# A macaron block: both expert layers as one group of eight steps, two biases moved, the last joins shared by two engines

## The chip, the cores and the metric

One core of a Trainium2 chip runs the whole program in one launch. The metric is the device time of an execution in microseconds (us), here always of that one core; a lower time is better. The engines are TensorE (PE), VectorE (DVE), ScalarE (ACT), GpSimd (POOL) and SyncE (SP). SP and POOL issue the transfers between device memory and the core.

## The reference

Input: 32 tiles of 128 tokens (8 sequences of 512), 128 features, f32.

```python
x = x + 0.5 * ffn(layernorm(x))           # layer 0
x = x + attention(layernorm(x))
x = x + 0.5 * ffn(layernorm(x))           # layer 1, the same weights

# ffn: a second layernorm, then top 2 of 8 experts per token by softmax(normed @ router.T);
#   each expert: silu(gate) * up @ down, 384 wide; and a shared expert, 128 wide, for all tokens
# attention: windows of 128 tokens; q, k, v = x @ W.T + b; scores q k / sqrt(128); in each row the
#   32 largest of 128 scores kept, softmax, times v; leaky relu; + its input; layernorm * gamma + beta
```

## The kernel before

**Steps and blocks.** The 32 tiles are worked on in 8 steps of 4 tiles (`TB`). In a step of an expert layer the router picks two experts for each token, VectorE works out a row number for each of the 1024 (token, expert) pairs (`s_idx`, line 1316), and POOL scatters the normed tokens to those rows of a table `rows` in device memory, eight indirect transfers for a step (line 1726), so that the rows of one expert stand together. The expert's work is then done in blocks of 128 rows of one expert: SP loads the rows (line 519) and the expert's weights (line 522); TensorE transposes (line 793), multiplies for gate (800), up (809) and down (820); ScalarE copies the transpose (1049), makes silu of the gate (1052) and copies the output (1058); VectorE multiplies silu by up (1543); POOL scatters the 128 output rows to `results` (line 1747). A block has four parts (0 transpose, 1 gate, 2 up, 3 down), and each engine has those of its own.

**Lists and groups.** Which expert a block belongs to is known only at run time. VectorE writes lists of blocks (`block_list`, lines 1373 to 1429) from the counts of the steps so far, and `level` (1364) keeps the counts at the steps named in `LEVELS`, by which a list is put in order, so that results of early steps come early. A list can be worked on once the steps it covers are scattered (`begin`, line 482). `GROUPS` says which steps share a region of `rows`: a group pays for one partly filled block for each expert, so its last list has seven blocks more than the rows need at best. `FIRST`, the first block of each list, comes to 0, 31, 78, 87, ..., 127, 149: layer 0 has a list of 31 blocks (steps 0 to 2) and one of 47 (steps 3 to 7), layer 1 seven lists with 71 blocks. `RUNS` are the places where the pipeline of blocks is drained: 31, 78 and the end. At a group's end SP writes pads over the unfilled rows (`fill_all`, 529; `fill_spare`, 465). Outputs stand in 12 buffers (`YB`); the load of block B waits until the result of block B - 12 is scattered.

**The order.** Every engine runs a written order. Between the pieces of the routing and attention steps stands a call `turn()`, and the numbers in `WEAVE` say for each engine how many block parts it does at each call (`z3` is three calls with none). For TensorE: first the eight routing steps of layer 0 (`first_turn` to `first_prefixes`), then for s in `TURNS` a step that holds, for four tiles each, attention of step a, the rest of attention of step a - 1 (`turn_p`, `mix`), routing of layer 1 of step a - 2 (`turn_z`, line 655, `logits`, `prefixes`), and the transpose of the next step's attention input (`turn_x`, line 647). What is left of the blocks comes behind all steps (`turn.rest()`).

**Around the change.** After layer 0's blocks of some steps are stored, SP loads their results (`stored`, `results`, lines 539 and 559), ScalarE multiplies the rows by their gates (`gate_rows`, line 956, a turn behind each second row) and VectorE adds them to the stream (`combine`, line 1457). `values` (TensorE, line 694) multiplies by the weights; VectorE adds the bias `bv_b` to a 128x512 tile (line 1500). `biased` adds the bias of attention's last norm to the stream (POOL, line 1737, ahead of that step's routing scatters). At the end of layer 1 all results of steps 0 to 6 are weighted by ScalarE and added by VectorE; those of the last step are weighted and added in one operation on VectorE (`last_joins`, line 1461).

Of the kernel before, what the change touches and what calls it, by code (L numbers as in the profile page):

```python
# [120 lines left out]
for now, f in zip(SHARED_AT, TURNS):  # L121
# [23 lines left out]
        z160 1 z4 1 z6 1 z5 1 z3 1 z3 1 z2 1 z4 1 z8 1 z5 1 z7 1 z4 1 z1 1 z5 2 z7 1 z2 1 z2 1 z3 1 z7 1 z1 1 z1 3 14 z5 1 z10 2 z1 1 z1 1 z10 1 2
        z16 1 z12 1 z3 1 z7 1 z6 1 z2 1 z4 1 z13 1 z18 2 1 z8 1 z7 1 z1 1 z6 1 z5 1 z15 1 1 z28 1 z4 1 z6 1 z15 2 z20 1 z24 1 z14 1 z2 1 1 z5 1 z10
        1 z4 1 z22 1 z40 1 z2 1 z15 1 z1 1 z9 1 z17 1 z7 1 z21 1 z1 1 z15 1 1 z15 1 z7 1 z1 1 1 z25 1 z2 1 z31 1 z1 1 z5 1 z16 1 z5 1 z2 1 z5 1 z16
        1 z18 1 z16 1 1 z7 1 z12 1 z4 1 z7 1 z30 1 z15 1 z5 1 z8 1 z11 2 1 z31 1 z2 1 z7 1 z4 2 z4 2 z1 3 16 3 2 z2 1 z10""",
# [6 lines left out]
VALUES, AFTER, AFTER_LATE, PICKS, SHARED, SHARED_LATE = 8, 13, 12, 19, 26, 31  # L155
# [48 lines left out]
def macaron(nc, x, wq, bq, wk, bk, wv, bv, ga, ba, gf, bf, rw, guw, dnw, sguw, sdnw, out, xs, yt):  # L204
    ctx = ExitStack()
    with ctx:
# [150 lines left out]
        cb, gated = sem("cb"), sem("gated")  # L357
# [569 lines left out]
        def _(act):  # L927
# [57 lines left out]
            def mix(A):  # L985
# [141 lines left out]
            for J in range(LAST_LO):  # L1127
                gate_rows(STEPS + J, yg_of(STEPS + J), J * TB)
# [10 lines left out]
        def _(dve):  # L1139
# [483 lines left out]
            for s, f in enumerate(TURNS):  # L1623
# [8 lines left out]
                if R is not None:  # L1632
                    stats_route(R, Jr, rt)

                def between(m):
# [3 lines left out]
                    if m == VALUES and a is not None:  # L1639
                        values(a)  # L1640
# [147 lines left out]
```

## Time and profile before

| | us |
|---|---|
| median of three executions | 546.54 |
| lowest, highest | 544.11, 551.48 |
| the profiled execution | 548.3 |
| its span in the profile | 546.5 |
| TensorE busy | 468.9 |
| VectorE busy | 368.8 |
| ScalarE busy | 348.1 |
| POOL busy | 288.6 |

The page gives the busy time of each engine over the whole span; the timeline gives single instructions with the idle time of the engine before them and, in brackets, what ended it; the windows cut the span into stretches with the busy time of each engine and the clock that TensorE was granted there (1.00 is 2.4 GHz, half of it 1.2 GHz; a value between is a mean of the stretch). Times are counted from the start of the span.

### The profile page before, as it was taken

How to read it: one execution, taken by the hardware profiler on the slowest of the kernel's cores; microseconds unless marked ns; L12 is line 12 of the kernel's file. 1: busy time of each engine (PE TensorE's matmuls, PEld its weight loads, DVE VectorE, ACT ScalarE, POOL GpSimd, SP SyncE). 2: the span in 40 equal slices, each digit the busy share in tenths (PEclk: the TensorE clock that was granted, in tenths of full speed). 3: DMA queues.
4: the chain of work that ended last, by engine and by line, in shares of the span. 5: the costliest groups of instructions: out<-in, count | busy, mean ns of one | idle time of the engine just before them, and what ended most of it. 6: DMA issues, size and time to landing. Idle time of an engine off the chain costs nothing.

```text
span 546.5 us, 13689 instructions
## 1 busy us (share of the span) xinstructions
PE 468.9 (86%) x3662; PEld 427.8 (78%) x3662; DVE 368.8 (67%) x1660; ACT 348.1 (64%) x870; POOL 288.6 (53%) x320
## 2 busy tenths in 40 slices
PE   2496799889997999999989989989998999699960
PEld 1483699888897879798868778887978898699960
DVE  5455654574225578888999989999999967222245
ACT  3374356547458568677887776868665565655586
POOL 2357367777731543233474736284685777544431
PEclk9999798999999999999999989999999999999995
DMA  6962485667658545352844366455554456767787
GB/s 170 303 168 88 169 277 189 213 194 264 230 191 300 188 158 172 139 192 95 271 146 160 108 231 185 160 179 171 170 184 165 158 211 214 257 236 260 244 289 235
DMA packets 79399, 108.42 MB, mean 198 GB/s; under 512 B 10888, under 2 KB 54288, under 8 KB 79328
## 3 DMA queue, kind: packets, MB, share of 16 engines
q1 hardware_dynamic: 68048, 88.33, 48.7%
q0 software_dynamic: 8864, 18.24, 10.2%
q10 hardware_dynamic: 2416, 0.99, 0.8%
q8 instruction: 34, 0.56, 0.4%
q14 instruction: 37, 0.30, 0.2%
HBM read 25.64 MB, written 23.29 MB: 90 GB/s over the span
## 4 chain that ended last, share of the span: by engine, by line
PE 44%; DVE 23%; issue 9%; ACT 9%; DMA 8%; SPq 4%; POOL 1%; ACTq 0%; DVEq 0%; POOLq 0%
PE ps_y L820 10%; PE ps_g L800 10%; PE ps_u L809 5%; PE ps_h L809 5%; DMA raw_dn<-in_dnw 3%; DVE raw_gu L1543 2%; DVE scores L1520 2%; PE w L686 2%; ACT yg L956 2%; DVE top L1515 2%; PE ps_x L793 2%; DVE bn L1163 2%; DMA yg<-results 2%; SPq L475 2%; DMA results<-raw_gu 2%
## 5 line engine op out<-in xcount | busy, mean ns | idle before, releaser
L1747 POOL DMA_INDIRECT results<-raw_gu x149 | 147.5, 990 | 133.6 <-ACT raw_gu L1058 96.1
L1726 POOL DMA_INDIRECT rows<-zz,s_idx x128 | 125.7, 982 | 93.1 <-issue 48.9
L820 PE MATMUL ps_y<-dn_t,raw_gu 128*128 x894 | 128.1, 280 | 10.5 <-ACT raw_gu L1058 9.7
L800 PE MATMUL ps_g<-x_t,raw_dn 128*128 128x128 f32 x894 | 127.3, 279 | 0.0
L820 PEld LDWEIGHTS ps_y<-dn_t,raw_gu 128*128 128x128 f32 x894 | 113.1, 193 | 17.6 <-issue 17.3
L800 PEld LDWEIGHTS ps_g<-x_t,raw_dn 128*128 128x128 f32 x894 | 113.7, 194 | 2.2 <-issue 2.2
L1052 ACT ACTIVATE sil<-ps_g 128x384 f32<-128x384 f32 x149 | 73.3, 492 | 17.5 <-PE ps_g L800 16.9
L1058 ACT COPY raw_gu<-ps_y 128x128 f32<-128x128 f32 x149 | 39.4, 264 | 69.2 <-PE ps_y L820 68.8
L1049 ACT ACTIVATE x_t<-ps_x,bf_c,gf_c 128x128 f32<-128x128 f32 x149 | 68.9, 462 | 21.8 <-PE ps_x L793 21.8
L1543 DVE TENSOR_TENSOR raw_gu<-sil,ps_h 128x384 f32<-128x384 f32 x74 | 40.7, 550 | 49.5 <-PE ps_h L809 34.9
L809 PE MATMUL ps_u<-x_t,raw_dn 128*128 128x128 f32 x450 | 64.1, 280 | 2.3 <-DVE raw_gu L1543 2.3
L1543 DVE TENSOR_TENSOR raw_gu<-sil,ps_u 128x384 f32<-128x384 f32 x75 | 41.2, 550 | 36.8 <-PE ps_u L809 30.2
L809 PE MATMUL ps_h<-x_t,raw_dn 128*128 128x128 f32 x444 | 62.1, 276 | 0.0
L809 PEld LDWEIGHTS ps_u<-x_t,raw_dn 128*128 128x128 f32 x450 | 58.0, 196 | 5.0 <-DVE raw_gu L1543 3.1
L809 PEld LDWEIGHTS ps_h<-x_t,raw_dn 128*128 128x128 f32 x444 | 55.8, 192 | 2.3 <-issue 1.7
L793 PE MATMUL ps_x<-ident,raw_gu 128*128 128x128 f32 x149 | 41.7, 280 | 12.3 <-DMA raw_gu<-rows 11.5
L973 ACT ACTIVATE zz<-xres,nmr,rstd 128x256 f32<-128x256 f32 x64 | 34.8, 595 | 8.7 <-DVE nmr L1230 8.7
L1515 DVE MAX8 top<-scores 128x8 f32<-128x128 f32 x128 | 35.3, 285 | 0.8 <-ACT scores L1019 0.8
L1520 DVE MATCH_REPLACE8 scores<-top,scores 128x128 f32<-128x128 f32 x128 | 34.9, 275 | 0.0
L793 PEld LDWEIGHTS ps_x<-ident,raw_gu 128*128 128x128 f32 x149 | 21.5, 144 | 16.3 <-issue 14.8
L956 ACT ACTIVATE yg<-yg,gates 128x128 f32<-128x128 f32 x96 | 30.8, 400 | 4.1 <-DMA yg<-results 4.1
L1457 DVE TENSOR_TENSOR xres<-xres,yg 128x512 f32<-128x512 f32 x24 | 16.9, 705 | 12.1 <-ACT yg L956 11.7
(228 smaller groups left out, 690.9 us busy)
## 6 DMA issues: line engine op xcount, KB each, us to landing
raw_dn<-gu_t SPq DMA_DIRECT2D x149, 384.0 KB
raw_gu<-rows SPq DMA_DIRECT2D x149, 64.5 KB, 2.8
yg<-results SPq DMA_DIRECT2D x12, 512.0 KB, 4.3
results<-raw_gu POOLq DMA_INDIRECT x149
rows<-zz,s_idx POOLq DMA_INDIRECT x128
out<-xres SPq DMA_DIRECT2D x7, 256.0 KB, 3.5
rows<-pads SPq DMA_DIRECT2D x24, 64.5 KB
raw_dn<-in_dnw SPq DMA_DIRECT2D x1, 1536.0 KB, 15.1
```

The source lines that it names most:

```text
L793: pe.transpose(ps_x[:, 0, :], xin[:, kx, 0:D], ident[:]).then_inc(xT_ps, 1)
L800: t = pe.matmul(ps_g[k][:, c, :], ws[:, k4, c * P:(c + 1) * P], x_t[:, k, :], start=True, stop=True)
L809: t = pe.matmul(ps_us[k][:, c, :], ws[:, k4, FF + c * P:FF + (c + 1) * P], x_t[:, k, :], start=True, stop=True)
L820: t = pe.matmul(ps_y[:, 0, :], h_t[:, k4, c * P:(c + 1) * P], dn[:, bass.ds(off + c * D, D)], start=(c == 0), stop=(c == FC - 1))
L956: act.activation(yg[n][:, k, c, :], yg[n][:, k, c, :], ACT.Copy, scale=gates[:, c, tile + k:tile + k + 1]).then_inc(gated, 1)
L1049: act.activation(x_t[:, k, :], ps_x[:, 0, :], ACT.Identity, bias=bf_c[:], scale=gf_c[:]).then_inc(xT_sb, 1)
L1052: act.activation(sil[:, B % 3, :], ff(ps_g[k]), ACT.Silu).then_inc(sil_done, 1)
L1515: dve.max(top[:, k, eight], src[:, k, :]).then_inc(tk, 1)
L1520: dve.match_replace(wk_s[:, k, :], top[:, k, eight], src[:, k, :], TAKEN).then_inc(tk, 1)
L1543: dve.tensor_tensor(h_t[:, k4, :], sil[:, B % 3, :], ff(ps_us[k]), ALU.mult).then_inc(h_done, 1)
L1726: pool.indirect_dma_start(xs, bass.IndirectOffsetOnAxis(s_idx[n][:, c, k:k + 1], 0), zz[n][:, k, c, :], None).then_inc(scat[n], 16)
L1747: pool.indirect_dma_start(yt, bass.IndirectOffsetOnAxis(xin[:, ky, D:D + 1].bitcast(I32), 0), yb[:, ky, :], None).then_inc(yst[ky], 16)
```

## The change

- `GROUPS`: layer 0's eight steps are one group. Its lists end at steps 2, 3 and 8, with 9, 8 and 54 blocks, 71 for 78; `LEVELS` of the group are 3, 4, 6 and 8. `FIRST` becomes 0, 9, 17, 71, 80, ..., 120, 142, `RUNS` 0, 71, 142. One drain, one pair of pad writes and one copy between groups fall away. All tables of `WEAVE` are written anew.
- `values`: TensorE adds the bias itself, by a second matmul into the same sum with a contraction of one row; ScalarE copies the sum.
- `biased` moves from POOL to VectorE, at the start of its step there.
- ScalarE norms step 0's attention input ahead of weighting step 1's results, and has a turn behind each weighted row.
- The last joins: of layer 1's steps 0 to 6, the odd ones go on as before, the even ones are weighted and added in one operation on VectorE, eight for a step, with a new semaphore between the two halves.

Cut to its core (of `WEAVE` POOL's and SP's tables alone):

```diff
-GROUPS = ((3, 5), (8,))
-LISTS = ((3, 8), (2, 3, 4, 5, 6, 7, 8))
-LEVELS = (3,), (4, 6, 8), (7, 8)
+GROUPS = ((8,), (8,))
+LISTS = ((2, 3, 8), (2, 3, 4, 5, 6, 7, 8))
+LEVELS = (3, 4, 6, 8), (7, 8)
...
     "sp": """
-        z2 12 28 z1 37 2 6 25 23 3 28 z1 2 81 4 46 z1 1 z9""",
+        32 z1 45 2 8 12 23 2 26 7 18 57 5 46 1 z10""",
...
     "pool": """
-        z34 1 z1 2 z2 1 1 z2 1 z1 1 z2 1 z6 1 1 z4 1 1 1 2 z1 3 1 z3 13 6 2 22 2 z1 1 z5 3 1 z2 2 z1 1 1 z1 1 4 z3 1 1 z4 1 3 z1 1 z7 7 z7 6 1 3 z8
-        6 1 1 z6 6 z8 4""",
+        z34 2 1 1 z31 1 z2 16 36 1 z2 1 1 z1 1 z2 2 z5 1 1 6 z2 1 z2 1 1 z1 1 z1 4 2 z4 2 1 2 z2 1 1 z2 4 2 z6 1 2 5 z2 1 z4 6 1 z7 10""",
...
+        def scalar_gates(C):
+            return C < STEPS or C % 2 == 1
...
                 for k in range(TB):
-                    t = pe.matmul(w1[:, k, :], xn_t[:, k, :], wv_t, start=True, stop=True)
+                    pe.matmul(w1[:, k, :], xn_t[:, k, :], wv_t, start=True, stop=False)
+                    t = pe.matmul(w1[:, k, :], one_f[0:1, :], bv_b[0:1, :], start=False, stop=True)
                 t.then_inc(v_ps, 1)
...
                         act.activation(yg[n][:, k, c, :], yg[n][:, k, c, :], ACT.Copy, scale=gates[:, c, tile + k:tile + k + 1]).then_inc(gated, 1)
-                        if k % 2:
-                            turn()
+                        turn()
...
+            def values(a):
+                act.wait_ge(v_ps, a + 1)
+                act.copy(v[:], w1[:]).then_inc(v_sb, 1)
...
                 if a in ALONE:
                     gate_rows(a, yg_of(a), a * TB)
+                if a in ALONE:
+                    norm_x(a, chain_alone[a])
                 if p is not None:
                     gate_rows(p, yg_of(p), p * TB)
                 if a in ALONE:
-                    norm_x(a, chain_alone[a])
                     turn_x(a)
...
                 if A is not None:
                     mix(A)
+                    turn()
+                if a is not None:
+                    values(a)
                     turn()
...
             for J in range(LAST_LO):
-                gate_rows(STEPS + J, yg_of(STEPS + J), J * TB)
+                if scalar_gates(STEPS + J):
+                    gate_rows(STEPS + J, yg_of(STEPS + J), J * TB)
...
             def combine(C, n, tile):
 
+                if not scalar_gates(C):
+                    dve.wait_ge(yld[n], 16 * loads_of_yg(C))
+                    before_this = TB * sum(not scalar_gates(c) for c in range(C))
+                    for c in range(2):
+                        for k in range(TB):
+                            if c:
+                                dve.wait_ge(halves, before_this + k + 1)
+                            t = dve.scalar_tensor_tensor(res(tile, k), yg[n][:, k, c, :], gates[:, c, tile + k:tile + k + 1],
+                                                         res(tile, k), ALU.mult, ALU.add)
+                            if not c:
+                                t.then_inc(halves, 1)
+                            elif k:
+                                t.then_inc(cb, 1)
+                            turn()
+                    return
...
+            def biased(A):
+
+                dve.wait_ge(xn_done, A * TB + TB)
+                xr = xres[:, A * TB:A * TB + TB, :]
+                dve.tensor_tensor(xr, xr, wide(ba_b), ALU.add).then_inc(xb_done, 1)
+                turn()
...
-            def values(a):
-                dve.wait_ge(v_ps, a + 1)
-                dve.tensor_tensor(v[:], w1[:], bv_b[:].rearrange("p (o d) -> p o d", o=1).broadcast_to([P, TB, D]),
-                                  ALU.add).then_inc(v_sb, 1)
...
                     stats_route(R, Jr, rt)
+                if A is not None:
+                    biased(A)
...
-                    if m == VALUES and a is not None:
-                        values(a)
...
-            def biased(A):
-
-                pool.wait_ge(xn_done, A * TB + TB)
-                xr = xres[:, A * TB:A * TB + TB, :]
-                pool.tensor_tensor(xr, xr, wide(ba_b), ALU.add).then_inc(xb_done, 1)
-                turn()
...
-                if A is not None:
-                    biased(A)
```

## Rows read from the trace of the kernel before

**Rows 1.** The page, busy microseconds, share of the span and instructions of each engine.

```profile
PE 468.9 (86%) x3662; PEld 427.8 (78%) x3662; DVE 368.8 (67%) x1660; ACT 348.1 (64%) x870; POOL 288.6 (53%) x320
```

**Rows 2.** Timeline of TensorE, blocks alone; start, duration, engine, line, operation, tiles, count.

```profile
132.73 0.27 PE L793 MATMUL ps_x<-ident,raw_gu 128*128 128x128 f32 x1
132.84 0.83 PE L800 MATMUL ps_g<-x_t,raw_dn 128*128 128x128 f32 x6
...
134.85 0.27 PE L793 MATMUL ps_x<-ident,raw_gu 128*128 128x128 f32 x1
```

**Rows 3.** Windows: stretch, length, busy PE PEld DVE ACT POOL, PEclk, DMA, GB/s.

```profile
57.00:70.00 13.00, 9.77 (x65) 9.44 (x66) 8.66 (x35) 5.84 (x13) 6.54 (x7) 0.74 0.62 211
265.00:430.00 165.00, 152.18 (x1181) 136.34 (x1181) 156.78 (x811) 120.42 (x297) 99.29 (x102) 0.99 0.51 170
```

**Rows 4.** Timeline of POOL and of SP's loads; in brackets idle time and releaser.

```profile
53.98 0.97 POOL L1726 DMA_INDIRECT rows<-zz,s_idx  x1 [0.30 <-issue]
...
57.06 0.37 SPq L519 DMA_DIRECT2D raw_gu<-rows  x1
...
61.64 0.97 POOL L1726 DMA_INDIRECT rows<-zz,s_idx  x1 [6.69 <-DVE s_idx L1316]
62.91 0.96 POOL L1726 DMA_INDIRECT rows<-zz,s_idx  x1 [0.30 <-issue]
```

**Rows 5.** Timeline of VectorE, the first two lists of blocks.

```profile
38.65 0.16 DVE L1355 CAST ends<-run 128x8 int32<-128x8 f32 x1
...
42.50 0.24 DVE L1418 TENSOR_SCALAR table<-be 128x31 int32<-128x31 int32 x1
...
113.39 1.33 DVE L1411 TENSOR_TENSOR scores<-blk_row,bend 128x1128 f32<-128x1128 f32 x1 [0.20 <-DVE bend L1410]
...
120.30 0.19 DVE L1418 TENSOR_SCALAR table<-be 128x47 int32<-128x47 int32 x1
```

**Rows 6.** Timeline of TensorE: a restart, block 17 and the first attention transpose.

```profile
61.79 2.08 PE L759 MATMUL ps_h<-sm_t,sh 128*128 128x128 f32 x8 [2.49 <-DVE sh L1298]
...
110.52 0.27 PE L793 MATMUL ps_x<-ident,raw_gu 128*128 128x128 f32 x1
...
176.06 0.60 PE L647 MATMUL w<-ident,xn 128*128 128x128 f32 x4
```

**Rows 7.** Groups by line: count | busy us, mean ns | idle before, releaser.

```profile
L1543 DVE TENSOR_TENSOR raw_gu<-sil,ps_u 128x384 f32<-128x384 f32 x75 | 41.2, 550 | 36.8 <-PE ps_u L809 30.2 <-ACT sil L1052 6.2
L1737 POOL TENSOR_TENSOR xres<-xres,ba_b 128x512 f32<-128x512 f32 x8 | 10.2, 1278 | 21.2 <-ACT xn L964 21.1
L694 PE MATMUL w<-sm_t,xn_t 128*128 128x128 f32 x64 | 8.7, 280 | 0.0
L1500 DVE TENSOR_TENSOR v<-w,bv_b 128x512 f32<-128x512 f32 x8 | 5.5, 692 | 1.5 <-PE w L694 1.3
L655 PE MATMUL w<-ident,zz 128*128 128x128 f32 x32 | 5.0, 278 | 2.3 <-ACT zz L973 2.3
L983 ACT COPY pr_t<-w 128x512 f32<-128x512 f32 x8 | 4.8, 594 | 1.5 <-PE w L628 1.5
```

**Rows 8.** Timeline of the tail, ScalarE, TensorE and VectorE.

```profile
522.96 1.86 ACT L956 ACTIVATE yg<-yg,gates 128x128 f32<-128x128 f32 x6 [1.46 <-DMA yg<-results]
...
532.05 1.65 PE L820 MATMUL ps_y<-dn_t,raw_gu 128*128 x6 [1.57 <-ACT raw_gu L1058]
...
541.99 2.19 DVE L1461 SCALAR_TENSOR_TENSOR xres<-raw_gu,gates,xres 128x128 f32<-128x128 f32 x8
```

**Rows 9.** The page's DMA issues: KB of each, median us to landing.

```profile
raw_gu<-rows SPq DMA_DIRECT2D x149, 64.5 KB, 2.8
```

**Rows 10.** Timeline of POOL, SP and TensorE, layer 1's last list.

```profile
465.11 0.97 POOL L1726 DMA_INDIRECT rows<-zz,s_idx  x1 [0.31 <-issue]
...
469.63 0.37 SPq L519 DMA_DIRECT2D raw_gu<-rows  x1
...
474.45 0.30 PE L793 MATMUL ps_x<-ident,raw_gu 128*128 128x128 f32 x1 [3.14 <-DMA raw_gu<-rows]
```

More of the change, by code:

```diff
@@ L134 @@
     "sp": """
-        z2 12 28 z1 37 2 6 25 23 3 28 z1 2 81 4 46 z1 1 z9""",
+        32 z1 45 2 8 12 23 2 26 7 18 57 5 46 1 z10""",
     "pe": """
-        z3 1 1 z2 3 3 z9 1 1 3 14 2 6 9 2 z1 10 z2 11 4 102 3 z1 2 1 11 2 z1 2 1 2 2 3 1 6 2 7 2 z1 1 2 2 2 10 z1 2 7 9 3 2 1 2 2 5 z1 2 1 4 2 5 1 1
-        z2 2 5 1 4 z1 10 2 7 1 z3 1 2 2 5 1 4 5 7 1 z3 3 6 z1 11 z1 3 4 10 z1 2 z2 2 5 1 3 1 1 5 10 3 1 7 2 1 7 11 1 1 4 z1 23 3 2 3 z1 6""",
+        z4 3 z2 1 4 z4 1 z2 2 z1 3 z1 10 8 4 2 5 z1 1 14 z1 2 6 1 108 4 1 2 4 4 1 z1 2 2 2 2 3 z1 1 3 4 1 z1 2 2 2 3 3 z1 2 4 8 1 z3 2 5 z1 2 z1 2 4
@@ L139 @@
+        5 z1 1 z2 2 7 z1 6 1 3 3 8 1 z3 1 4 1 7 1 3 4 8 2 z3 1 5 z1 3 1 5 6 7 2 z3 2 5 1 2 z1 2 6 8 3 1 10 z1 3 2 18 3 2 4 z1 23 3 2 4 z1 19""",
     "act": """
-        z11 1 z5 1 6 z13 2 3 3 1 2 4 z1 3 2 1 5 1 z1 4 z2 1 1 1 1 23 4 50 z3 3 1 z1 1 3 z3 3 2 1 1 6 z3 2 2 z1 2 3 z5 1 1 z1 3 z1 2 5 z3 2 2 z2 5 z2
-        1 z1 3 2 z1 1 z2 5 5 z1 1 2 1 z3 2 z1 4 z1 1 1 1 z3 2 z3 2 1 4 3 z7 1 z1 1 1 z1 2 z4 2 2 z1 3 z1 3 4 5 1 z8 2 z2 1 1 1 z2 4 z3 2 z1 3 4 1 z8
-        1 2 z1 4 z2 1 z1 5 2 1 1 1 z1 4 3 3 z1 1 z4 1 z1 3 z2 2 z1 1 z1 1 5 1 z1 6 z1 1 z1 5 z1 1 3 1 z2 5 7 3 z3 2 2 z1 18 z3 3 2 z1 13 9 66 z2 2 1
@@ L143 @@
-        1 z2 2 z3 1 z5 1 z10""",
+        z12 1 z4 1 6 z6 1 z2 3 1 z2 1 6 1 z2 1 6 z2 5 z2 1 1 z1 7 z1 1 2 z1 6 2 64 z4 3 z2 8 z3 2 z2 1 1 1 z3 2 z1 3 3 z4 1 2 1 z1 5 z5 1 z8 1 3 z4
+        2 1 z1 3 4 z7 1 z4 1 z1 3 4 z3 2 z2 1 z2 1 z1 2 z1 2 z6 2 z5 1 z1 3 4 z8 1 z2 2 1 2 z4 1 1 z2 4 z2 3 z1 1 2 2 4 z2 1 z7 2 z1 1 2 z3 6 z7 1
+        z1 2 4 2 z2 1 z1 1 z4 1 1 1 1 z1 1 z3 3 z1 1 z2 2 1 z2 4 2 2 z1 1 z1 1 1 z4 2 1 z1 2 z3 1 5 z1 1 4 2 z1 1 z1 4 z1 3 z2 1 z1 8 6 6 z3 2 3 z1
+        19 z3 3 3 1 14 6 69 z3 2 z3 1 z2 1 z2 1 z10""",
@@ L144 @@
     "dve": """
[L145 to L148, printed above, removed]
+        z170 1 z5 1 z6 1 z1 1 z15 1 z3 2 z13 1 z3 1 1 z2 1 z7 1 z5 2 1 z34 11 z1 2 9 1 z6 1 z7 2 1 1 z1 1 z11 1 z6 1 z7 1 z15 1 z17 1 z13 1 1 z10 1
@@ L149 @@
+        z14 1 z17 1 z7 1 z1 1 z25 1 z21 1 z6 1 z8 1 z9 1 z11 1 z13 1 z28 1 z6 1 z5 1 z1 1 z4 1 z21 1 z5 1 z13 1 z35 1 z1 1 z13 1 z14 1 z7 1 z17 1 1
+        z29 1 z6 1 z13 1 z2 1 z17 1 1 z14 1 z3 1 z34 1 z10 1 z14 1 z7 1 z3 1 z4 1 z2 1 z19 1 z18 1 z4 1 z11 1 z4 1 z9 1 z7 1 z11 1 z5 1 z27 2 z20 1
+        1 z9 1 z11 1 z2 1 z1 1 z16 1 z11 1 z6 1 1 1 z9 1 z1 2 1 z1 19 z3 2 z3 1 z1 1 z28""",
     "pool": """
-        z34 1 z1 2 z2 1 1 z2 1 z1 1 z2 1 z6 1 1 z4 1 1 1 2 z1 3 1 z3 13 6 2 22 2 z1 1 z5 3 1 z2 2 z1 1 1 z1 1 4 z3 1 1 z4 1 3 z1 1 z7 7 z7 6 1 3 z8
@@ L151 @@
-        6 1 1 z6 6 z8 4""",
+        z34 2 1 1 z31 1 z2 16 36 1 z2 1 1 z1 1 z2 2 z5 1 1 6 z2 1 z2 1 1 z1 1 z1 4 2 z4 2 1 2 z2 1 1 z2 4 2 z6 1 2 5 z2 1 z4 6 1 z7 10""",
 }
-VALUES, AFTER, AFTER_LATE, PICKS, SHARED, SHARED_LATE = 8, 13, 12, 19, 26, 31
+AFTER, AFTER_LATE, PICKS, SHARED, SHARED_LATE = 13, 12, 19, 26, 31
 EXTRA, EXTRA_JOINS, EXTRA_LATE = 18, 23, 27
@@ L355, in macaron @@
             sem(n) for n in ("tl", "tl_e", "bl", "ended", "tab", "gts", "run0", "padded"))
-        cb, gated = sem("cb"), sem("gated")
+        cb, gated, halves = sem("cb"), sem("gated"), sem("halves")
         yld = [sem(f"yld{n}") for n in range(4)]
@@ L1450, in combine @@
             def combine(C, n, tile):
+                if not scalar_gates(C):
[13 more added lines that the diff above has]
+                    return
                 xr = xres[:, tile:tile + TB, :]
+                before_this = sum(scalar_gates(c) for c in range(C))
                 for c in range(2):
-                    dve.wait_ge(gated, (2 * C + c + 1) * TB)
+                    dve.wait_ge(gated, (2 * before_this + c + 1) * TB)
                     if c:
@@ L1479, in leaky, with wide @@
                 turn()
+            def wide(t):
+                return t[:].rearrange("p (o d) -> p o d", o=1).broadcast_to([P, TB, D])
+            def biased(A):
[3 more added lines that the diff above has]
+                turn()
             def scaled(k, A):
```

2 lines of the change are left out of this document (removed).

## The prediction

> **What bounds the kernel now.** I read the page's busy times first: TensorE works for 86% of the span, VectorE for 67% [rows 1]. Next the timeline of TensorE in a stretch of blocks alone: one expert block begins 2.12 us after the one before it, with 19 instructions (one transpose and three groups of six), 0.11 us each [rows 2]. Then the windows, since a share of the whole span hides stages. From 265 to 430, most of the eight attention steps, TensorE is busy for 152.2 of 165 us and VectorE for 156.8 [rows 3]: there a shorter step has two engines to get past. Before the first attention transpose at 176.06 [rows 6] the order is TensorE's, with POOL as its supplier: no list of blocks can start before POOL has scattered its rows, and POOL issues one scatter each 1.27 us (62.91 less 61.64, [rows 4]). At the end ScalarE weights result rows, and the copies of block outputs queue among them [rows 8]. So the change is costed in three stretches: to the first attention transpose, from there to the last list, and the tail.
>
> **Part 1, the groups: when the big list of layer 0 arrives.** Before, block 31 was the first to need routing steps 3 to 7, and 31 blocks (steps 0 to 2, the last scatter over at 54.95 [rows 4]) fed TensorE meanwhile. After, the lists of layer 0 hold 9, 8 and 54 blocks; the third needs all eight steps, and only 17 blocks stand before it.
>
> POOL sets its earliest time. Step 3's first scatter was issued at 61.64 [rows 4]. VectorE now writes two short lists ahead of step 3's indices instead of one. The one took from 38.65 to 42.74 [rows 5], 4.1 us; the two have the same operations on fewer cells, an estimated 3.3 and 3.4, and a level is 0.4: +3 us, so 64.6. After that POOL's written order holds 40 scatters and only 6 result scatters: 46 x 1.27 = 58.4. One of the six waits for an output that is not there yet, an estimated 1.3. POOL is done at 124.3. VectorE's list of 54 blocks is written about then: the 47-block list was there at 120.49, four of its operations taking 1.33 us on 1128 cells [rows 5]; they now have 54 x 32 = 1728 cells, 0.7 more each. From the end of the first group's scatters to the first load of their rows it was 57.06 - 54.95 = 2.1 us [rows 4], and a load lands after 2.8 in the median; in the nearest single case it was 4.8 from issue to TensorE [rows 9, 10]. The buffer of block 17 waits also for block 5's result, which POOL issues right behind the run of scatters, 1.27 more. So TensorE begins block 17 at 124.3 + 2.1 + 1.3 + 2.8 = 130.5, of which I take 130. Bounds: 125 with scatters from 61.64 and no wait for an output, 134 with the slow load.
>
> Before, block 17 began at 110.52 [rows 6]; little in the order ahead of it changes, so TensorE stands for some 19 us. It restarts slowly: around a stop of 2.49 us the stretch 57 to 70 shows a granted clock of 0.74 [rows 3, 6], a lack of 0.26 x 13 = 3.4 us of full speed; I take 2.5 (bounds 0 and 3.4). By the written orders 101 parts, four to a block, lie between block 17 and the first attention transpose: 25.25 x 2.12 = 53.5. That transpose comes at 130 + 2.5 + 53.5 = 186, against 176.06: **+9.9**. The drain at block 31, which the change removes, lies inside the time that this replaces.
>
> **Part 2, the blocks that are gone.** Layer 0 has 71 blocks for 78. TensorE's written order has 271 parts for 301 between the first attention transpose and the last step's routing transpose: 7.5 blocks, 7.5 x 2.12 = **-15.9** if TensorE sets those steps. If VectorE does, only its products are saved, 7.5 x 0.55 [rows 7] = -4.1. I take TensorE: its share is 92% where VectorE's is 95% [rows 3], and what VectorE's products wait for is mostly TensorE's up matmuls, 30.2 us in half of them [rows 7].
>
> **Part 3, the values' bias.** TensorE gets four matmuls of one contraction row per step, eight instructions like the eight of the values themselves (64 in eight steps, [rows 7]): 64 x 0.11 = 7.1. No row shows a contraction of one row; bounds 0 and the 8.7 of busy time that the 64 have [rows 7]; I take the nearest row's. Right behind them TensorE waits for ScalarE's normed rows, 2.3 us in all eight steps [rows 7], which the new matmuls fill: 7.1 - 2.3 = **+4.8**. The Trainium skill, "TensorE: Matmul & The Clock Gate", Step-by-step, says that loading the stationary operand takes time by its columns and that its row count does not matter. By that the lower bound of 0 goes and the 7.1 stay; no run shown has such a matmul. Eight additions of 692 ns leave VectorE, and eight copies like L983's of 594 ns come to ScalarE [rows 7], busy there for 120 of 165 us [rows 3], which covers them; uncovered they cost 4.8 (rival E).
>
> **Part 4, attention's bias.** POOL's eight additions of 1278 ns go to VectorE, which did the values' on the same tile in 692 [rows 7]: what values give back it pays here, 0. POOL waited 21.1 us ahead of these additions, nearly all before the first [rows 7], and result scatters stood behind it; what TensorE lost by that is little: **-0.7** (an estimate, bounds 0 and -1.5). ScalarE's first attention norm now stands ahead of step 1's weighting; blocks cover that, and a turn after each weighted row instead of each second adds no work.
>
> **Part 5, the tail.** The last wait of TensorE for ScalarE's copy of an output is 1.57 us [rows 8]; with two such waits before it and the last copy I count 5.8, all because ScalarE is weighting rows. Four of the seven steps now skip that: 32 x 0.31 = 9.9 us off ScalarE [rows 8]. For each VectorE has eight fused operations of 2.19 together [rows 8] in place of two additions of about 0.69: 4 x 2.19 + 3 x 1.38 + 2.19 for the last step = 15.1 us of joins. From the first rows, at 522.96, that ends at 538.1 without a wait; with 2.5 for loads and products between them 540.6, against 544.18 [rows 8]: **-3.6** (bounds 0 and -5.8). The first load of the last list has one block part less ahead of it: **+0.5**.
>
> **Sum.** 9.9 - 15.9 + 4.8 - 0.7 - 3.6 + 0.5 = -5.0. The profiled execution took 548.3, 1.8 over its span and 1.8 over the median of 546.54: its own time goes to 543.3, and the same step off the median gives 541.5.
>
> **The rivals.** A is the sum above; by the bounds of part 1's start and of the tail its own range is 534.5 to 549.
>
> B: the third list is early. If step 3's scatters start at 61.64 as before and the restart costs nothing, TensorE is at block 17 at 125 and at the transpose at 178.5: +2.4 in place of +9.9, 534.0. For it: VectorE has fewer products to do ahead of 110. Against it: the clock fell around a far shorter stop.
>
> C: VectorE sets the steps. Its place is 265 to 430, its price that part 2 gives 4.1 and the bias matmuls are hidden: 9.9 - 4.1 - 0.7 - 3.6 + 0.5 = +2.0, 548.5. The change loses as soon as the stretch from the first attention transpose to the last step's shortens by less than 6.1. For it: 156.8 of 165 us [rows 3]. Against it: no work is added to VectorE there, and products go.
>
> D, the other side: the third list is late. One more wait in POOL's or SP's order will do, such as the pads that SP now writes behind block 15's weights, and TensorE has nothing else to do. From 135 on the change loses, from 146 on by over 2%; middle 141, 552.5. For it: in layer 1 TensorE got its rows 8.4 us after the last scatter (474.45 less 466.08, [rows 10]), where I allow 6.2. Against it: that list had other loads and writes ahead.
>
> E: ScalarE is late with the copied values, which stand in its order ahead of the next step's norms: 8 x 0.594 = 4.8, so 546.3. For it: the norms are what TensorE waits for already [rows 7]. Against it: 45 us of idle time in that stretch [rows 3]. The Trainium skill, "ScalarE: Activation LUTs", Rules for kernel authors, wants additions and products on VectorE and calls it up to about three times faster in bf16. Here, in f32, the trace differs: 594 ns on ScalarE for the tile that took 692 on VectorE; at three times 692 the eight copies would be an estimated 16.6 us of ScalarE, not 4.8.
>
> **How the numbers follow.** Chances: A 0.43, B 0.24, C 0.15, D 0.13, E 0.05. The time is A's. A change of 2%, about what a measurement of this kernel can tell from none, ends at 535.6 and 557.5. Faster holds 0.2 of B and 0.04 of A, 0.24; slower 0.06 of D and 0.02 of C, 0.08; the rest is 0.68. The range of 530 to 555 leaves out the lower end of B and the upper of D, about 0.15.
>
> **What would show it.** Part 1: a stop of TensorE of 15 to 23 us that ends at 125 to 134 with the clock at its lower level behind it, and the transpose of line 647 at 182 to 190. Part 2: from there to the last routing transpose 8 to 13 us less than before; under 6 is C. Part 3: 128 instructions where L694 has 64, 16 to 18 us, and copies of about 594 ns on ScalarE, no longer wait of TensorE for norms. Part 4: additions of about 692 ns on VectorE. Part 5: no wait of TensorE over 1 us after 520, and VectorE the last engine. A stop of TensorE that is missing, begins before 105 or ends after 140 makes the prediction wrong.

## The result: slower by 0.9%, and the profile after

| | before | after |
|---|---|---|
| median, us | 547.41 | 552.41 |
| lowest, highest | 544.11, 551.48 | 550.15, 556.97 |
| profiled execution, its span | 548.3, 546.5 | 553.1, 551.1 |

The ratio is 1.0087, 95% interval 1.0068 to 1.0105. The prediction was 541.5, a gain of 5; the time lies inside its range of 530 to 555, but the change went the other way. Lines of the kernel after are some 2 to 32 higher than those of before: blocks have lines 796, 803, 812 and 823, the attention transpose 649, the routing transpose 657, the values 696, their bias 697, POOL's scatters 1758.

Two instants cut both spans into the prediction's three stretches: the first attention transpose (X0) and the last step's routing transpose (Z).

| stretch, us | before | after | difference | predicted |
|---|---|---|---|---|
| start to X0 | 176.1 | 186.0 | +9.9 | +9.9 |
| X0 to Z | 270.0 | 266.8 | -3.2 | -11.8 (-15.9, +4.8, -0.7) |
| Z to the end of the span | 100.4 | 98.3 | -2.1 | -3.1 |

Z in the timeline of TensorE, before and after (start, duration, engine, line, operation, tiles, count):

```profile
446.08 0.60 PE L655 MATMUL w<-ident,zz 128*128 128x128 f32 x4
452.82 0.60 PE L657 MATMUL w<-ident,zz 128*128 128x128 f32 x4
```

So what is missing is missing in the middle, in the attention steps. First the stretch ahead of them. The timeline of POOL, SP and TensorE after (start, duration, engine, line, operation, tiles, count, and in brackets the idle time before and its releaser):

```profile
61.44 0.96 POOL L1758 DMA_INDIRECT rows<-zz,s_idx  x1 [9.71 <-DVE s_idx L1327]
...
115.66 0.96 POOL L1769 DMA_INDIRECT results<-raw_gu  x1 [0.30 <-issue]
...
119.45 0.95 POOL L1758 DMA_INDIRECT rows<-zz,s_idx  x1 [0.30 <-issue]
...
118.11 0.35 SPq L521 DMA_DIRECT2D raw_gu<-rows  x1
...
124.17 0.36 SPq L521 DMA_DIRECT2D raw_gu<-rows  x1
...
103.27 0.85 PE L618 MATMUL w<-ident,raw_sm 128*128 128x128 f32 x3
120.75 0.45 PE L796 MATMUL ps_x<-ident,raw_gu 128*128 128x128 f32 x1 [16.63 <-DMA raw_gu<-rows]
...
126.30 0.30 PE L796 MATMUL ps_x<-ident,raw_gu 128*128 128x128 f32 x1 [1.24 <-DMA raw_gu<-rows]
...
186.04 0.60 PE L649 MATMUL w<-ident,xn 128*128 128x128 f32 x4
```

POOL issues without a break up to 120.4, TensorE stands for 16.6 us, and block 17 (126.30) starts 15.8 us later than before [rows 6]. The long stop ends with block 16, still of the second list (120.75): its load, at 118.11, had to wait until the result of block 4 was scattered, and that scatter stands within POOL's run (115.66). Block 17, the first of the third list, waits 1.24 us more. Now the windows: stretch, length, busy time of PE, PEld, DVE, ACT and POOL, granted clock, share of DMA, GB/s.

```profile
120.00:126.00 6.00, 4.31 (x19) 4.04 (x19) 0.55 (x1) 2.62 (x5) 4.48 (x6) 0.54 0.39 134
224.00:228.00 4.00, 4.00 (x22) 4.00 (x23) 3.96 (x21) 2.65 (x7) 0.76 (x2) 0.57 0.05 16
265.00:430.00 165.00, 159.27 (x1198) 141.46 (x1198) 150.97 (x810) 121.03 (x301) 86.37 (x92) 0.98 0.51 168
280.00:285.00 5.00, 5.00 (x36) 5.00 (x35) 4.96 (x25) 4.20 (x11) 2.07 (x3) 0.74 0.37 122
```

From 265 to 430 VectorE has gone from 156.8 to 151.0 us, TensorE from 152.2 to 159.3 [rows 3], though there are fewer blocks. And the granted clock falls to 0.57 and 0.74 in places where TensorE is busy without a gap. Before, it was 1.00 in nearly all of these steps and fell once, behind a stop: TensorE was busy for 1.93 of the four us from 316.1, and the clock was 0.64 in the four behind them. The groups by line say where TensorE's time went (columns as in [rows 7]):

```profile
L697 PE MATMUL w<-bv_b,one_f 1*128 1x128 f32 x64 | 15.5, 321 | 0.0
L696 PE MATMUL w<-sm_t,xn_t 128*128 128x128 f32 x64 | 14.9, 315 | 0.0
...
L657 PE MATMUL w<-ident,zz 128*128 128x128 f32 x32 | 4.9, 276 | 0.0
...
L1515 DVE TENSOR_TENSOR xres<-xres,ba_b 128x512 f32<-128x512 f32 x8 | 5.4, 674 | 0.0
...
L996 ACT COPY v<-w 128x512 f32<-128x512 f32 x8 | 4.7, 586 | 22.6 <-PE w L697 22.6
```

The values' own 64 instructions had 8.7 us of busy time before [rows 7]; they have 14.9 now, and the 64 one-row ones 15.5 beside them. The timeline of one step's values, and of the block part behind them:

```profile
195.01 0.39 PE L696 MATMUL w<-sm_t,xn_t 128*128 128x128 f32 x2
195.33 0.48 PE L697 MATMUL w<-bv_b,one_f 1*128 1x128 f32 x2
195.75 0.49 PE L696 MATMUL w<-sm_t,xn_t 128*128 128x128 f32 x2
196.16 0.48 PE L697 MATMUL w<-bv_b,one_f 1*128 1x128 f32 x2
...
198.24 0.94 PE L823 MATMUL ps_y<-dn_t,raw_gu 128*128 x6
```

A pair of instructions begins every 0.42 us, where pairs at 0.11 an instruction [rows 2] would begin every 0.22: 16 instructions take 198.24 - 195.01 = 3.23 us, against an expected 1.8.

### The profile page after: what moved, and what is told of

It is laid out like the page before. It is cut to its first block, busy times and chain, and to the rows that moved or that the text cites. A ratio compares the mean times of both kernels' runs of the same rounds, so it can differ in the third digit from the quotient of the medians.

```text
span 551.1 us, 13347 instructions
## 1 busy us (share of the span) xinstructions
PE 471.3 (86%) x3593; PEld 425.2 (77%) x3593; DVE 368.6 (67%) x1694; ACT 332.5 (60%) x823; POOL 269.7 (49%) x304
## 4 chain that ended last, share of the span: by engine, by line
PE 62%; DMA 11%; ACT 7%; issue 7%; DVE 7%; POOL 3%; SPq 2%; ACTq 0%; POOLq 0%; DVEq 0%
PE ps_g L803 13%; PE ps_y L823 13%; PE ps_h L812 6%; PE ps_u L812 6%; DMA raw_dn<-in_dnw 3%; POOL rows L1758 3%; PE w L697 2%; PE ps_x L796 2%; PE w L688 2%; DMA yg<-results 2%; PE w L710 2%; PE w L696 2%; DMA results<-raw_gu 2%; DMA rows<-zz,s_idx 1%; PE w L673 1%
## 5 line engine op out<-in xcount | busy, mean ns | idle before, releaser
L1769 POOL DMA_INDIRECT results<-raw_gu x142 | 137.9, 971 | 171.9 <-ACT raw_gu L1064 133.3
L823 PE MATMUL ps_y<-dn_t,raw_gu 128*128 x852 | 124.0, 283 | 7.9 <-ACT raw_gu L1064 7.2
L803 PE MATMUL ps_g<-x_t,raw_dn 128*128 128x128 f32 x852 | 121.5, 280 | 0.0
L823 PEld LDWEIGHTS ps_y<-dn_t,raw_gu 128*128 128x128 f32 x852 | 109.0, 195 | 13.8 <-issue 12.9
L803 PEld LDWEIGHTS ps_g<-x_t,raw_dn 128*128 128x128 f32 x852 | 108.9, 195 | 3.0 <-issue 3.0
L1058 ACT ACTIVATE sil<-ps_g 128x384 f32<-128x384 f32 x142 | 69.9, 492 | 15.4 <-PE ps_g L803 14.7
L812 PE MATMUL ps_u<-x_t,raw_dn 128*128 128x128 f32 x426 | 60.9, 280 | 0.6 <-DVE raw_gu L1575 0.6
L812 PEld LDWEIGHTS ps_u<-x_t,raw_dn 128*128 128x128 f32 x426 | 54.9, 196 | 3.0 <-issue 1.4
L959 ACT ACTIVATE yg<-yg,gates 128x128 f32<-128x128 f32 x80 | 26.1, 395 | 6.6 <-DMA yg<-results 6.6
L1174 DVE BATCH_NORM_STATS2 bn<-xres 128x6 f32<-128x128 f32 x96 | 20.4, 279 | 2.3 <-DMA xres<-in_x 2.0
```

Of the source, the lines that this page charges most:

```text
L803: t = pe.matmul(ps_g[k][:, c, :], ws[:, k4, c * P:(c + 1) * P], x_t[:, k, :], start=True, stop=True)
L812: t = pe.matmul(ps_us[k][:, c, :], ws[:, k4, FF + c * P:FF + (c + 1) * P], x_t[:, k, :], start=True, stop=True)
L823: t = pe.matmul(ps_y[:, 0, :], h_t[:, k4, c * P:(c + 1) * P], dn[:, bass.ds(off + c * D, D)], start=(c == 0), stop=(c == FC - 1))
L1058: act.activation(sil[:, B % 3, :], ff(ps_g[k]), ACT.Silu).then_inc(sil_done, 1)
L1769: pool.indirect_dma_start(yt, bass.IndirectOffsetOnAxis(xin[:, ky, D:D + 1].bitcast(I32), 0), yb[:, ky, :], None).then_inc(yst[ky], 16)
```

## Experiments

Times are compared with the kernel before, run beside them (medians of 547.1 to 548.1), and with the kernel after (552.4). X0 moves between 186 and 191 in profiles of kernels that are alike up to there, so the stretches are compared from X0 on.

### The form of the bias matmul

Theory R: the one-row matmuls between full ones are what is dear. Theory V is the prediction's rival C: VectorE sets the steps. Theory S: two matmuls into one sum wait for each other.

**e1_full_rows.** The same sum, with 128 contraction rows in place of one:

```diff
-                    t = pe.matmul(w1[:, k, :], one_f[0:1, :], bv_b[0:1, :], start=False, stop=True)
+                    t = pe.matmul(w1[:, k, :], ident[:], bv_b[:], start=False, stop=True)
```

> The values' bias is added by a matmul of 128 contraction rows (the identity as one operand, the bias in every row as the other) in place of one row; the result is the same. Theory R (the one-row matmuls between full ones are slow: in the changed kernel a step's 16 instructions take 3.3 us, 0.21 each, where full ones take 0.11): a step's 16 take 1.8, 8 x 1.5 = 12 us less, and up to 4.5 more if the stretches of lower clock behind them go: 536 to 541, beside 552.4. Theory V (VectorE sets the steps): 551 to 553. Theory S (a second matmul into a sum just begun has to wait for the first): no gain in these instructions, 552.

Measured: 540.99 (540.72 to 541.29), ratio to before 0.9871 (0.9808 to 0.9934). The timeline of the same place:

```profile
194.70 0.39 PE L696 MATMUL w<-sm_t,xn_t 128*128 128x128 f32 x2
194.92 0.39 PE L697 MATMUL w<-bv_b,ident 128*128 128x128 f32 x2
195.14 0.39 PE L696 MATMUL w<-sm_t,xn_t 128*128 128x128 f32 x2
...
196.48 0.83 PE L823 MATMUL ps_y<-dn_t,raw_gu 128*128 x6
```

A pair begins every 0.22 us, and a step's sixteen take 1.78. X0 to Z takes 254.7 us for 266.8, with X0 at 186.0 in both; Z is here:

```profile
440.67 0.60 PE L657 MATMUL w<-ident,zz 128*128 128x128 f32 x4
```

Its windows have a granted clock of 1.00 where the kernel after has 0.57 and 0.98 (columns as above):

```profile
224.00:228.00 4.00, 3.78 (x19) 2.54 (x19) 3.53 (x23) 2.87 (x7) 0.96 (x1) 1.00 0.39 131
265.00:430.00 165.00, 157.15 (x1254) 142.10 (x1253) 156.36 (x832) 122.11 (x305) 94.80 (x101) 1.00 0.52 174
```

The number of rows of the bias matmul makes 11.4 us. S falls, since the two sums still depend on each other; V alone falls, since VectorE's work is the same.

**e3_apart, e5_wide.** One-row matmuls kept, but apart from the full ones: four behind the four, or a single one of 512 columns ahead of them.

```diff
                 for k in range(TB):
-                    pe.matmul(w1[:, k, :], xn_t[:, k, :], wv_t, start=True, stop=False)
-                    t = pe.matmul(w1[:, k, :], one_f[0:1, :], bv_b[0:1, :], start=False, stop=True)
+                    pe.matmul(w1[:, k, :], xn_t[:, k, :], wv_t, start=k == 0, stop=False)
+                for k in range(TB):
+                    t = pe.matmul(w1[:, k, :], one_f[0:1, :], bv_b[0:1, :], start=False, stop=k == TB - 1)
```

> The four full matmuls of a step first, then the four one-row matmuls together; same result. Theory R with the cost at each change between a full and a one-row matmul: 16 x 0.11 plus two changes of 0.2, 2.2 us for 3.3: 543 to 545, less if the clock stays up. Theory R with the cost in the one-row matmul itself (0.21 each): 2.6 for 3.3: 546 to 547. Theory V: 552.

```diff
+                pe.matmul(w1[:], one_f[0:1, :], bv_b[0:1, :].rearrange("p (o d) -> p o d", o=1).broadcast_to([1, TB, D]),
+                          start=True, stop=False)
                 for k in range(TB):
-                    pe.matmul(w1[:, k, :], xn_t[:, k, :], wv_t, start=True, stop=False)
-                    t = pe.matmul(w1[:, k, :], one_f[0:1, :], bv_b[0:1, :], start=False, stop=True)
+                    t = pe.matmul(w1[:, k, :], xn_t[:, k, :], wv_t, start=False, stop=k == TB - 1)
```

> The changed kernel with one one-row matmul of 512 columns that begins the sum of a whole step, then the four full matmuls: one change between one row and 128 in a step where the changed kernel has eight. If each change costs, a step's values take 2.0 to 2.4 us for 3.3, and the time is that of the full-row form, 539 to 543. If a one-row matmul costs by itself, by its columns, the step takes 2.7 or more: 545 to 548.

Measured: 542.11 (ratio 0.9888, 0.9813 to 0.9963) and 542.59 (0.9919, 0.9891 to 0.9947). The timeline of e3_apart:

```profile
196.18 1.06 PE L696 MATMUL w<-sm_t,xn_t 128*128 128x128 f32 x8
197.16 1.15 PE L698 MATMUL w<-bv_b,one_f 1*128 1x128 f32 x8
198.25 0.94 PE L824 MATMUL ps_y<-dn_t,raw_gu 128*128 x6
```

Eight one-row instructions take 1.09 with one change at each end; sixteen take 2.07. In e5_wide the step's ten instructions take 2.05. So the price is paid at each change between the row counts: eight in a step after, two here.

**e6_half_rows.** 64 rows, alternating as in the kernel after (bias/64 in 64 equal terms):

```diff
-                    t = pe.matmul(w1[:, k, :], one_f[0:1, :], bv_b[0:1, :], start=False, stop=True)
+                    t = pe.matmul(w1[:, k, :], half_f[0:64, :], bv_b[0:64, :], start=False, stop=True)
```

> The changed kernel with the bias matmul over 64 contraction rows (64 equal terms of bias/64), alternating with the full ones as in the changed kernel; same result but for rounding. If any change of the number of rows costs as one row does: 0.21 us an instruction, 552. If only the very thin form costs: 0.11, 541.

Measured: 550.08 (ratio 1.0034, 1.0002 to 1.0067). The pairs are as slow as with one row:

```profile
200.15 0.48 PE L698 MATMUL w<-bv_b,half_f 64*128 64x128 f32 x2
200.56 0.49 PE L697 MATMUL w<-sm_t,xn_t 128*128 128x128 f32 x2
200.98 0.48 PE L698 MATMUL w<-bv_b,half_f 64*128 64x128 f32 x2
```

It is the change that costs, not the thinness. But the granted clock stays at 1.00 from X0 to Z here; X0 to Z takes 263.2, and the kernel is 2.3 us faster than the one after. The fall of the clock without a gap came only with one row in the alternating order: behind three of the eight steps' values in the kernel after and four of eight in f_before_one_row below. With one row and two changes (e3_apart) the clock stayed at 1.00 too.

### Which engine sets the steps

**e2_no_bias, e4_vector_values.** The bias matmul left out; then the values as before, VectorE adding the bias.

```diff
-                    pe.matmul(w1[:, k, :], xn_t[:, k, :], wv_t, start=True, stop=False)
-                    t = pe.matmul(w1[:, k, :], one_f[0:1, :], bv_b[0:1, :], start=False, stop=True)
+                    t = pe.matmul(w1[:, k, :], xn_t[:, k, :], wv_t, start=True, stop=True)
...
                 if a is not None:
-                    values(a)
                     turn()
...
+                    if m == 8 and a is not None:
+                        values(a)
```

(the second and third part in e4_vector_values alone, on ScalarE and VectorE)

> The values' bias is left out altogether, ScalarE still copies the sum: the output lacks it. Theory R: a step has 2.4 us less, 8 x 2.4 = 19.5, and 0 to 4.5 of clock: 528 to 533. By the prediction's own price of 0.9 per step: 545. Theory V: 551 to 553.

> The values as before the change: no bias matmul, VectorE adds the bias while it copies (8 x 0.69 us), ScalarE's copy goes; all else is the changed kernel, with attention's bias on VectorE too. Theory R: 528 to 535. Theory V: 552 + 5.5 = 557, as VectorE has more work than in the changed kernel.

Measured: 540.57 (ratio 0.985, 0.9778 to 0.9922) and 548.54 (0.9979, 0.9935 to 1.0022). Without any bias matmul the kernel is no faster than with the full-row one: 64 full instructions of 0.11, 7.1 us of TensorE, cost nothing that can be measured here. Eight additions on VectorE, 5.5 us, cost 8.0 by the medians, but executions of e4_vector_values lie between 541.5 and 549.7, and in its one profile X0 to Z takes 258.2 for 255.7, so 2.5 is what can be traced to the steps. From 265 to 430 VectorE is busy for 156.4 of 165 us in e1_full_rows and 155.8 without the bias matmul, TensorE for 157.2 and 152.5. That points to VectorE as what holds the steps once TensorE's slow pairs are out of the way, as rival C said; no run shows it by making VectorE's work alone shorter. The expectation of 528 to 535 for both missed that: it took the whole of TensorE's saving off the path.

### The values' part alone, on the kernel before

**f_before_one_row, f2_before_full_row.** The kernel before with the values' part of the change, ScalarE copying and VectorE's addition gone, in the two forms.

```diff
-                    t = pe.matmul(w1[:, k, :], xn_t[:, k, :], wv_t, start=True, stop=True)
+                    pe.matmul(w1[:, k, :], xn_t[:, k, :], wv_t, start=True, stop=False)
+                    t = pe.matmul(w1[:, k, :], one_f[0:1, :], bv_b[0:1, :], start=False, stop=True)
...
+                if a is not None:
+                    values(a)
...
-                    if m == VALUES and a is not None:
-                        values(a)
```

(f2_before_full_row: `ident[:], bv_b[:]`)

> The kernel before with the values' part of the change alone: one-row bias matmuls and ScalarE's copy, VectorE's addition gone. Theory R: 8 x 2.4 = 19.5 us more of TensorE, of which the waits for norms (2.3) and the 5.5 us taken from VectorE give some back: 555 to 564 beside 547. The prediction's price of 0.9 a step: 552. If VectorE sets the steps whatever TensorE does: 542.

> The kernel before with the values' part alone, but the bias matmul with 128 contraction rows. The one-row form alone came to 568 (+20). At the prediction's price, 0.9 us a step less the 2.3 that it hides, 4.8: 552. If VectorE, relieved of 5.5 us, sets the steps of before: 542. If only the one-row form were dear and the rest nil: 547.

Measured: 568.16 (ratio 1.0382, 1.0293 to 1.0471) and 553.55 (1.0097, 1.0056 to 1.0137). X0 to Z: 288.5 and 272.4, for 270.0 before. With 7.5 more blocks in the steps TensorE has no room, and the one-row form costs 20 us, 14.6 of them by its form alone. The full-row form costs 6.1 by the medians; in its one profile 3.8 of 6.6 lie ahead of X0, where none of its instructions has run, and X0 to Z takes 2.4 more, half of the 4.8 that the prediction gave.

### POOL's run of scatters

**i_pool_late.** Full-row bias; in POOL's order eight result scatters moved from behind routing step 7's scatters to ahead of them:

```diff
-        z34 2 1 1 z31 1 z2 16 36 1 ...
+        z34 2 1 1 z26 8 z4 1 z2 8 36 1 ...
```

> The changed kernel with the full-row bias (541.0), and in POOL's order eight result scatters moved from behind step 7's scatters to ahead of them. If POOL's run of scatters sets the third list's start, as the prediction has it, each us there is one of the end: 8 x 1.27 = 10.2 later, the first attention transpose at 196 for 186, 551. If SP's pads or its loads set it: 541 to 543.

Measured: 554.79 (ratio 1.0147, 1.0062 to 1.0233), 13.8 over e1_full_rows. TensorE's waits and X0 in its timeline:

```profile
114.15 0.45 PE L796 MATMUL ps_x<-ident,raw_gu 128*128 128x128 f32 x1 [10.47 <-DMA raw_gu<-rows]
...
136.28 0.44 PE L796 MATMUL ps_x<-ident,raw_gu 128*128 128x128 f32 x1 [18.06 <-DMA raw_gu<-rows]
...
197.80 0.60 PE L649 MATMUL w<-ident,xn 128*128 128x128 f32 x4
```

Block 17 starts at 136.28 for 126.11 in e1_full_rows: 8 x 1.26 = 10.1 us of POOL are 10.2 of TensorE. So close an agreement is in part luck, as block 17 starts between 126.1 and 130.1 in profiles of kernels that are alike up to there; but the third list's start is POOL's. Block 16 comes 6.5 us earlier (114.15 for 120.61), since block 4's result is now scattered at 108.13: its wait and block 17's are two, and both are for POOL.

### The tail and attention's bias

**g_scalar_tail.** Full-row bias, and ScalarE weighting the rows of all seven steps as before:

```diff
         def scalar_gates(C):
-            return C < STEPS or C % 2 == 1
+            return True
...
-                    gate_rows(STEPS + J, yg_of(STEPS + J), J * TB)
+                    gate_rows(STEPS + J, yg_of(STEPS + J), J * TB, tail_turn)
...
-                    turn()
+                    for _ in range(TB if C >= STEPS and C % 2 == 0 else 1):
+                        turn()
```

(`tail_turn` is a turn behind three rows of seven, so that the written orders still fit; the tail of before had one behind each second row.)

> The changed kernel with the full-row bias (541.0) and the tail of before: ScalarE weights the rows of all seven steps, VectorE adds. The prediction put the new tail at -3.6: 544.6. By the changed kernel's stretch from the last routing transpose to the end, 98.3 for 100.4, it is worth 2.1: 543. If the tail is hidden: 541.

Measured: 545.41 (ratio 0.9949, 0.9909 to 0.999), 4.4 over e1_full_rows; Z to the end takes 101.8 for 98.1. The shared joins are worth some 4 us.

**h_pool_bias.** Full-row bias, and attention's bias back on POOL; 18 of its result scatters stand behind the first addition, so this is no pure undoing.

```diff
-        z34 2 1 1 z31 1 z2 16 36 1 ...
+        z34 2 1 1 z31 1 z2 34 18 1 ...
...
             for a, A, J, *_ in TURNS:
+                if A is not None:
+                    biased(A)
```

> The changed kernel with the full-row bias (541.0), attention's bias back on POOL, where it stood before the change; 18 of POOL's result scatters move behind the first of these additions, so that none of them waits for a later block. If VectorE sets the steps now (the run without any bias matmul gained nothing over the full-row one, the one with values on VectorE lost 7.5): 8 x 0.69 = 5.5 go, 533 to 537. If TensorE does: 541. If POOL's wait for the normed rows holds up results that blocks need: 543 or more.

Measured: 550.18 (ratio 1.0051, 1.0013 to 1.009), 9.2 over e1_full_rows; X0 to Z takes 264.6 for 254.7. Its list of waits (waiter, releaser, us in total, times, longest):

```profile
DVE xres L1523 <- POOL xres L1761: 7.0, 2, 4.4
```

VectorE waits 7.0 us for POOL's addition, and with the eight additions gone it is still busy for 230.4 us between X0 and Z, where e1_full_rows has 229.8. The timeline of the kernel before, which has the addition on POOL too, shows why. An operation of VectorE can be held until POOL's addition ends; that happens beside four of the eight additions, in both kernels, while the shorter steps of the search (MAX8, MATCH_REPLACE8) run on beside others.

```profile
280.26 1.29 POOL L1737 TENSOR_TENSOR xres<-xres,ba_b 128x512 f32<-128x512 f32 x1
...
279.83 1.87 DVE L1485 SCALAR_TENSOR_TENSOR rr<-rr,mv,ga_b 128x128 f32<-128x128 f32 x1
...
281.91 0.33 DVE L1485 SCALAR_TENSOR_TENSOR rr<-rr,mv,ga_b 128x128 f32<-128x128 f32 x1
```

The groups of this operation, before, in the kernel after and in h_pool_bias:

```profile
L1485 DVE SCALAR_TENSOR_TENSOR rr<-rr,mv,ga_b 128x128 f32<-128x128 f32 x32 | 12.8, 400 | 0.0
L1522 DVE SCALAR_TENSOR_TENSOR rr<-rr,mv,ga_b 128x128 f32<-128x128 f32 x32 | 10.7, 336 | 0.0
L1514 DVE SCALAR_TENSOR_TENSOR rr<-rr,mv,ga_b 128x128 f32<-128x128 f32 x32 | 11.9, 371 | 0.0
```

With others that are held in the same way, h_pool_bias has some 5 us more of such busy time than e1_full_rows, about as much as the 5.4 that it saves. The granted clock also fell behind stops of TensorE (0.89 from 400 to 432). How much of the 9.2 is the wait, the held operations, the clock or the moved result scatters was not told apart.

### The full-row form once more

**e1_again.** The kernel of e1_full_rows, measured again.

> The changed kernel with the full-row bias matmul once more, in more rounds, as the version that would beat both: 539 to 544 against the kernel before at 547, by the one cause found (the one-row form). If its first result was a lucky one: 545 to 549, as its X0 (the first attention transpose) moved between 186 and 190 in kernels alike up to there.

Measured: 541.02 (537.38 to 542.31), ratio 0.9879 (0.9831 to 0.9926). It beats before by 1.2% and after by 2.1%.

## Why the prediction was wrong

**The step that failed is part 3, the price of the bias matmul.** The prediction took "the nearest row's" 0.11 us an instruction and 7.1 for 64, with bounds of 0 and 8.7. Sixteen instructions of a step took 3.23 us where that makes 1.8, so the 64 new ones cost 8 x (3.23 - 0.90) = 18.6, over twice the upper bound (0.90 is what the values' own eight take at 0.11 each). The bounds came from how long a full matmul is busy; that the full ones around it become slow as well was in none of the bounds. The values' instructions were busy for 15.5 + 14.9 = 30.4 us, where the prediction's sign said 16 to 18. From X0 to Z the miss is 8.6 us (-3.2 for -11.8). The form costs 12.1 there (266.8 for 254.7): 8.5 of them come with the slow pairs alone (263.2 with 64 rows, where the clock stayed up), and the other 3.6 (2.3 by the medians) come where the clock fell behind such stretches (0.57 from 224 to 228). The remaining terms together came out 3.5 better than forecast.

With the form alone changed, the same kernel took 541.0 for a predicted 541.5. That closeness is partly luck: its stretches came to +9.9, -15.3 and -2.3 for +9.9, -11.8 and -3.1, and its gain by medians is 6.2 for 5.0.

**Part 1 was right in its sum, by luck.** X0 came at 186.04 for 186. Its terms missed on both sides: step 3's first scatter came at 61.44, not 64.6, as the two short lists delayed nothing; POOL's run held five result scatters, not six, and none of them waited; POOL was done at 120.4 for 124.3; from there to the load of block 17 it took 3.8 us for 3.4, and from the load to TensorE 2.1 for 2.8; block 17 began at 126.3 for 130 (bounds 125 to 134), and from it to X0 it took 59.7 for 56.0. TensorE did 26 blocks there and not 25.25, which makes 55.1 at 2.12 each, and waited three times, 0.54, 1.05 and 1.74 us, which the prediction put at nothing. The low clock, 0.54 from 120 to 126, fell on block 16; from 126.3 on it was 1.00, so the 2.5 for a slow restart was not spent behind block 17. The long stop began at 104.1, ahead of the 105 that was named as a sign of error, and ended at 120.75, not at 125 to 134: the prediction had block 17 wait for its list and missed that block 16 would wait for block 4's result in the same run of POOL. That POOL sets block 17's start was tested (i_pool_late) and holds.

**Part 2 held in size; its reason is not shown.** With the full-row bias X0 to Z fell by 15.3, where the prediction had 15.9 for the blocks and 0.7, less 4.8 for the bias, and the bias matmuls cost nothing (e2_no_bias). No run has the groups alone, so what the blocks gave stays open. TensorE was busy there for 243.7 us for 254.0 before, VectorE for 229.8 for 239.0. VectorE's 9.1 are more than the 4.1 of products that the prediction counted: about 5 of them are operations that POOL's additions no longer hold (h_pool_bias). The wait for norms that they were to fill did go, from 2.3 [rows 7] to 0.0.

**Part 4 was probably under-valued.** VectorE's additions took 674 ns for an expected 692, ScalarE's copies 586 for 594. The prediction took the exchange between values and attention's bias as even for VectorE; it left out that an addition on POOL also holds VectorE, about 5 us of busy time in the eight steps. What values gave back was worth 2.5 by the profile and 8.0 by the medians (e4_vector_values). What attention's bias was worth in time is not shown, as h_pool_bias is no pure undoing.

**Part 5 was near.** The joins were put at -3.6; against g_scalar_tail they gave -3.7 by the profiles and -4.4 by the medians, with other turns in that tail. From before to after the whole stretch fell by 2.1 for 3.1. In the kernel after, TensorE's waits behind 520 are all under 1 us, and VectorE is the last engine:

```profile
532.00 0.93 PE L823 MATMUL ps_y<-dn_t,raw_gu 128*128 x6 [0.72 <-ACT raw_gu L1064]
533.71 0.93 PE L823 MATMUL ps_y<-dn_t,raw_gu 128*128 x6 [0.77 <-ACT raw_gu L1064]
...
546.58 2.19 DVE L1488 SCALAR_TENSOR_TENSOR xres<-raw_gu,gates,xres 128x128 f32<-128x128 f32 x8 [1.84 <-DMA raw_gu<-results]
```

**The rivals.** C named 548.5 and its sign (X0 to Z shortened by 3.2, under 6.1; 6.8 with the 0.7 that lies there too) was met, but by another cause: VectorE was less busy there than before, TensorE more. B's early list came (block 17 at 126.3 for its 125), but not its early X0 (186.0 for 178.5). D was the fear for the third list, which came early rather than late. E did not come: ScalarE's copies waited 22.6 us for TensorE's pairs, not TensorE for them.

**The page on the row count.** The Trainium skill, "TensorE: Matmul & The Clock Gate", Step-by-step, says that the row count does not matter for a load of the stationary operand. For the load by itself the trace agrees: a pair of one-row loads takes as long as a pair of full ones. The weight loads of the kernel after:

```profile
194.91 0.30 PEld L696 LDWEIGHTS w<-sm_t,xn_t 128*128 128x128 f32 x2
195.33 0.29 PEld L697 LDWEIGHTS w<-bv_b,one_f 1*128 1x128 f32 x2
195.74 0.30 PEld L696 LDWEIGHTS w<-sm_t,xn_t 128*128 128x128 f32 x2
```

But the pair of loads at 195.33 begins with its own matmul, not ahead of it. In e1_full_rows each pair begins 0.11 us ahead of its matmul:

```profile
194.59 0.30 PEld L696 LDWEIGHTS w<-sm_t,xn_t 128*128 128x128 f32 x2
194.81 0.30 PEld L697 LDWEIGHTS w<-bv_b,ident 128*128 128x128 f32 x2
```

The rule was used to defend a price for the whole matmul, and it speaks of the load alone. What the trace shows lost is the load's head start, 0.11 us, while a pair begins 0.20 us later than with full rows; what makes the rest of it is not shown.

## What to carry to other kernels

Price a new matmul by its place in the stream as well as by its size: where its contraction rows differ from those of its neighbours, each change back and forth costs TensorE time in the neighbours too, so give it the neighbours' rows (an identity as the other operand cost nothing here) or put such matmuls together. A bound taken from a row of the same operation is a bound only for the same surroundings. When two engines are near their limits in a stretch, the saving on one is worth what the other leaves of it: 7.1 us of TensorE were worth nothing here, 5.5 us of VectorE between 2.5 and 8.0. When work moves from one engine to another, look also for the operations that ran beside it: they may have been held by it.

## What the runs showed of the hardware

- Alternating between 128 and 1 contraction rows, pairs of f32 matmul instructions begin every 0.42 us, for 0.22 with 128 throughout; with 64 rows it is the same 0.42. Eight one-row instructions in a row take 1.09 us, changes at both ends included.
- The granted clock fell (0.57 in 224 to 228, 0.74 in 280 to 285) while TensorE was busy without a gap, right behind the alternating one-row matmuls, in three steps of eight (four of eight in f_before_one_row). It stayed at 1.00 from X0 to Z with 64 rows at the same slow pace, with 128 rows (e1_full_rows), and with the one-row matmuls grouped.
- Operations of VectorE that run beside POOL's f32 addition of 128x512 (1.28 us) can be held until it ends, beside four of eight such additions in the kernel before and in h_pool_bias: one of 0.33 us took 1.87.
